# A two-layer gated cross-attention and expert network on one core: who normalises the rows for the second layer's routing

## What is computed

```python
x = x + jnp.tanh(g_xattn[1]) * _L1_xattn_ref(_layernorm(x), ctx_1024, mask, Wq, Wk, Wv, Wo)
x = x + jnp.tanh(g_ffn[1]) * _L1_ffn_ref(_layernorm(x), router_w, w1, w2)

def _layernorm(x, axis=-1, eps=1e-05):
    m = jnp.mean(x, axis=axis, keepdims=True)
    v = jnp.var(x, axis=axis, keepdims=True)
    return (x - m) / jnp.sqrt(v + eps)

# _L1_ffn_ref: 4096 tokens of width 128, 8 experts of width 512, 2 experts a token
logits = xf @ router_w.T
topv, topi = jax.lax.top_k(logits, 2)
topw = softmax(topv)
perm = xf[rev]                       # every token's row twice, sorted by expert
chunks = perm.reshape(e, n * k // e, d)
h = gelu(einsum('ecd,edf->ecf', chunks, w1))
y = einsum('ecf,efd->ecd', h, w2) * sw
out = zeros.at[rev].add(y)
```

## Time and profile before

| what | value |
|---|---|
| median of 3 runs | 753.41 us (750.35 to 755.98) |
| the profiled execution | 759.83 us |
| its span, first to last instruction | 758.3 us |
| busy in the span: TensorE, VectorE, ScalarE, GpSimd | 549.0, 416.8, 231.6, 330.2 us |
| mean granted clock of TensorE | 0.832 of full speed |

### The profile page before, as it was taken

How to read it: one execution, slowest core, us unless ns; L and a number is a source line. 1 busy time by engine, 2 the same in 40 slices (tenths; PEclk the granted TensorE clock), 3 DMA queues, 4 the chain that set the end, 5 groups by cost and what they waited for, 6 DMA issues and landing times.

```text
span 758.3 us, 16967 instructions
## 1 busy us (share of the span) xinstructions
PE 549.0 (72%) x5388; PEld 433.3 (57%) x5389; DVE 416.8 (55%) x1474; ACT 231.6 (31%) x411; POOL 330.2 (44%) x412
## 2 busy tenths in 40 slices
PE   1587957615699999972798887777861388999950
PEld 1356645501289999862354676666650166999950
DVE  4785386997523333314896467878568511222215
ACT  0221001123044444442622454454531021223210
POOL 6212104777535656634500000070747676666650
PEclk9967695865799999996799997786775699999995
DMA  7911000123222222412755164352324113222219
GB/s 199 269 42 32 26 14 30 49 96 99 74 75 82 77 79 74 140 45 68 238 185 175 51 167 109 108 159 51 70 64 129 46 54 103 79 81 77 72 56 311
DMA packets 70254, 74.97 MB, mean 99 GB/s; under 512 B 12216, under 2 KB 58552, under 8 KB 70120
## 3 DMA queue, kind: packets, MB, share of 16 engines
q1 hardware_dynamic: 55240, 49.64, 23.6%
q0 software_dynamic: 9968, 21.88, 9.2%
q10 hardware_dynamic: 4976, 2.53, 1.2%
HBM read 45.62 MB, written 28.29 MB: 97 GB/s over the span
## 4 chain that ended last, share of the span: by engine, by line
PE 51%; DVE 24%; POOL 8%; issue 8%; DMA 6%; ACT 1%; SPq 1%; POOLq 0%; DVEq 0%; ACTq 0%
PE PS L802 47%; POOL xs L543 5%; DVE XN L1406 3%; DVE stats L1385 3%; DMA work<-ys 3%; DVE X L1380 2%; PE PS L983 2%; DVE work L1845 2%; DVE work L1380 1%; POOL work L591 1%; DVE rtmp L1380 1%; DVE mv L1388 1%; DVE nwt L1380 1%; PE PS L1144 1%; POOL work L598 1%
## 5 line engine op out<-in xcount | busy, mean ns | idle before, releaser
L543 POOL DMA_INDIRECT xs<-pack,adr_i x80 | 78.2, 977 | 194.3 <-ACT pack L1219 138.5
L554 POOL DMA_INDIRECT ys<-work x136 | 132.6, 975 | 33.2 <-issue 33.2
L802 PE MATMUL PS<-w,work 128*128 x1088 | 137.4, 281 | 6.5 <-issue 6.4
L802 PEld LDWEIGHTS PS<-w,work 128*128 128x128 f32 x1088 | 129.4, 195 | 11.5 <-issue 10.2
L802 PE MATMUL PS<-work,w1h 128*128 128x256 f16 (+1 forms) x576 | 97.8, 271 | 3.4 <-issue 2.0
L802 PE MATMUL PS<-work 97*64 97x256 f16 (+5 forms) x608 | 75.7, 317 | 13.8 <-DVE work L1512 7.5
L1380 DVE TENSOR_TENSOR work<-PS,work 128x128 f32<-128x128 f32 (+3 forms) x82 | 32.0, 392 | 94.9 <-PE PS L802 50.6
L802 PE MATMUL PS<-work,w1l 128*128 128x256 f16 (+1 forms) x288 | 78.1, 272 | 0.0
L1277 ACT ACTIVATE work<-PS,b 128x256 f32<-128x256 f32 x128 | 50.3, 475 | 77.0 <-PE PS L802 77.0
L802 PEld LDWEIGHTS PS<-work 97*64 97x64 f16 (+2 forms) x608 | 57.7, 165 | 24.7 <-DVE work L1512 10.8
L802 PE MATMUL PS<-ones 128*128 128x512 f16 x195 | 50.7, 418 | 25.7 <-DVE rows_i L1642 12.4
(11 more groups left out here) (288 smaller groups left out, 858.8 us busy)
## 6 DMA issues: line engine op xcount, KB each, us to landing
work<-ys SPq DMA_DIRECT2D x12, 512.0 KB, 6.0
work<-xs SPq DMA_DIRECT2D x32, 130.0 KB
work<-xs SPq DMA_DIRECT2D x60, 65.0 KB
k_parts<-work SPq DMA_DIRECT2D x24, 128.0 KB, 2.1
w<-k_parts SPq DMA_DIRECT2D x8, 384.0 KB
work<-k_parts SPq DMA_DIRECT2D x32, 96.0 KB
work<-q_parts SPq DMA_DIRECT2D x8, 384.0 KB
work<-q_parts SPq DMA_DIRECT2D x32, 96.0 KB
```

What stands on the lines that cost most here:

```text
L543: g.indirect_dma_start(xs[l], bass.IndirectOffsetOnAxis(adr_i[:, k, T:T + 1], 0), pack_of(l, c)[:, s, k, :].bitcast(U32), None)\
L554: g.indirect_dma_start(ys[l], bass.IndirectOffsetOnAxis(xin[:, q, u, :].bitcast(U32)[:, D:D + 1], 0), yrow[:, q, u, :], None).then_inc(ff[ ...
L802: return t.matmul(o, lhsT, rhs, start=start, stop=stop, skip_group_check=True)
```

## The change

The rows of the second layer are no longer normalised by VectorE. GpSimd writes them for the first three groups (chunks 0 to 5) with the same two-step operation on X, mean and 1/std; each group stands in its queue ahead of the scatters of the group's first chunk. ScalarE writes them for the last two groups (chunks 6 and 7) with one activation a tile, x * (1/std) + shift, right before it copies the upper half. For that VectorE computes a shift, -mean/std, after each group's 1/std, and raises a new semaphore `scaled` with it. The first layer keeps its rows on VectorE, and the table of steps stays as it was.

```diff
+        shift_ = sb("shift_", [P, CT_TILES * 2])
...
+        scaled = sem("scaled")
...
+            def rows_normed(p):
+                t = group(1, p)
+                pool.wait_ge(scaled, p + 1)
+                if p >= 2:
+                    pool.wait_ge(pack_lo, NC + t.stop // CT_TILES - 4)
+                for s, T in enumerate(range(t.start, t.stop)):
+                    ins = g.tensor_scalar(XN[:, slots(1, t.start // CT_TILES).start + s, :], X[:, T, 0:D],
+                                          mv[:, T, 0:1], rstd[:, T:T + 1], ALU.subtract, ALU.mult)
+                    if s % CT_TILES == CT_TILES - 1:
+                        ins.then_inc(rt[1]["xn"], 1)
+
             for c in range(NC):
+                if c % 2 == 0 and c < NC - 2:
+                    rows_normed(c // 2)
                 if c < NC // 2:
                     for s in range(CT_TILES):
                         scatter(1, c, (s,))
...
                 for c in route_at("high", g):
+                    if c >= NC - 2:
+                        act.wait_ge(scaled, group_of(1, c) + 1)
+                        act.wait_ge(pack_lo, NC + c - 3)
+                        for s in range(CT_TILES):
+                            T = c * CT_TILES + s
+                            ins = a.activation(XN[:, slots(1, c).start + s, :], X[:, T, 0:D], ACT.Identity,
+                                               bias=shift_[:, s:s + 1], scale=rstd[:, T:T + 1])
+                        ins.then_inc(rt[1]["xn"], 1)
                     route_high(1, c)
...
             def route_rows_normed(l, p):
                 t = group(l, p)
-                if l == 1 and p >= 2:
-                    dve.wait_ge(pack_hi, NC + t.stop // CT_TILES - 4)
                 norm_rows(t, slots(l, t.start // CT_TILES).start, rt[l]["xn"])
...
                 for k in route_at("norm", g):
                     dve.wait_ge(x3_done, group(1, k).stop)
-                    norm_scale(group(1, k))
+                    t = group(1, k)
+                    norm_scale(t)
+                    v_.scalar_tensor_tensor(out=shift_[:, 0:width(t)], in0=mv[:, t, 0], scalar=-1.0, in1=rstd[:, t],
+                                            op0=ALU.mult, op1=ALU.mult).then_inc(scaled, 1)
                     route_lg(1, k)
                 for k in route_at("choose", g):
                     route_choose(1, k)
-                for k in route_at("normed", g):
-                    route_rows_normed(1, k)
```

## The result

The changed kernel took 759.5 us (median of 20 runs, 751.9 to 764.3) where the kernel before took 755.44 (20 runs, 750.35 to 760.13): ratio 1.0058, 95% interval 1.0035 to 1.0082. That is slower by 0.6%, inside the 1% that I called no change; the forecast was +2.0 us, and this comparison gives some +4. The profiled execution took 762.85 us with a span of 761.3 (before 759.83 and 758.3). Two later comparisons of the same kernel gave less; all runs together are at the end of the experiments.

What follows compares the result with a forecast made beforehand. From 561.27 us on, the end was taken to hang on when VectorE and ScalarE have chunk 4 packed. Shift +0.3, port +1.7 and the rest 0 gave +2.0 us on 753.41: 755.4 us, range 750.0 to 760.5.

Steps and rivals of the forecast that it cites:

- Rows removed from VectorE: Taking 32 tiles' normalisations off VectorE gains 0 us, since VectorE then waits for TensorE or GpSimd asks for the table later.
- Shift: One added VectorE instruction a group, before the logits, passed on for three groups at 0.1 us each: +0.3 us.
- GpSimd's normalisation: Each of 24 normalisations of 128 x 128 on GpSimd takes 0.3 us, bounds 0.2 and 1.27; they cost 0 themselves.
- The port: GpSimd's normalisations stretch VectorE's two-input instructions: 1.2 us in group 1's choice, 0.5 in group 0; +1.7 us, bounds 0 and 5.
- The rival that had GpSimd slow and VectorE held up: Each normalisation takes about 1.27 us and delays VectorE some 6 us in groups 0 and 1: 766 us; chance 0.1.
- Group 2 on time: GpSimd's group 2 rows are done at 554.3, some 3 us before ScalarE asks: 0 us.
- late rows: Above 0.7 us per normalisation, group 2 reaches ScalarE late and chunk 4 moves 1 to 2 us: 757 to 758; chance 0.05.
- ScalarE's eight activations: ScalarE's activations for the last two groups take 0.3 us each, 1.2 us for four, and cost 0.
- the idle time 2 us longer: Sign in the changed profile: VectorE idles 2 us longer ahead of each rank result.
- the scatters without a gap from chunk 4 on: Sign in the changed profile: GpSimd's scatters from chunk 4 on follow each other without idle time.
- a chunk 4 some 2 us later: Sign in the changed profile: GpSimd's scatters from chunk 4 on start about 2 us later.
- the change moves nothing: Rival: VectorE takes its turns with GpSimd without loss, leaving only the shift's 0.3 us: 753.7 us; chance 0.25.

Runs made afterwards that it cites:

- e9: The changed kernel measured a third time, with no further edit: 757.07 us (12 runs), ratio 0.9997 to the kernel before.
- e6: Changed kernel with four GpSimd two-input additions of 128 x 512 ahead of group 1's normalisations: 762.6 us (4 runs), ratio 1.0113 to the kernel before.
- e8: Changed kernel with GpSimd's batch for group 2 moved ahead of chunk 3's last four scatters: 760.59 us (12 runs), ratio 1.0051 to the kernel before.
- e1 to e4: Changed kernel again, GpSimd's part alone, ScalarE's part alone, changed kernel with group 2 back on VectorE: ratios 0.9990, 1.0026, 1.0007, 1.0009 to the kernel before.
- e5: Changed kernel with every GpSimd normalisation done twice, first into unread scratch: 760.62 us (6 runs), ratio 1.0100 to the kernel before.

## Why the prediction was right

The total was right, and its largest term was wrong. The measured 759.5 us lies 1.0 us inside the upper bound of 760.5, and 2.0 us of it are the kernel before's own: its median is 755.44 over 20 runs for the 753.41 of the three that I had.

- **Rows removed from VectorE: 0.** Right. The time came back as waits for TensorE in all three large groups (2.61 us to 4.57 in group 1), and the earlier table (597.86 for 599.23) was complete 6.5 us before GpSimd asked for it. In group 0 I had read 1.64 us of cover; with the 0.97 at 481.01 it was 2.61, so that the 0.5 us that I left open there had no ground.
- **Shift: +0.3.** Its size was right: 0.17 us long, the next instruction after 0.09 us (469.63 to 469.72). 0.3 us is below what any comparison here can tell.
- **GpSimd's normalisation: 0.3 us each.** This step failed; it is 0.80. I took the value nearest to the copy. The truth lies between the copy and the sum, inside the bounds of 0.2 and 1.27. A quarter of the sum's elements takes 0.63 of the sum's time, so dividing by elements was the mistake.
- **The port: +1.7.** This step failed. In the choice of group 1, where I had 1.2 us, it is 0 to 0.25 us, and in group 0, where I had 0.5, up to 0.4 (e9). The changed kernel's first profile has none in group 1. The two stretched rows that I had the earlier trace rows were both beside sums with two tensor inputs, and I carried them over to an instruction with one tensor and two scalars per row. e6 shows the difference inside one trace. The rival that had GpSimd slow and VectorE held up needed the port as well and was wrong with it: had the port acted for the whole of each instruction, 0.80 us each would have been near the 0.85 at which it decided the sign.
- **Group 2 on time: 0.** The slack was mis-sized, the price was not. I wrote that it holds up to 0.7 us for one instruction. At 0.80 the rows are late in four of six profiles, ScalarE waiting 0.80 to 1.67 us for them (0.8 us in the mean of the six). The rival "late rows" said so, and said that chunk 4 moves by 1 to 2 us. That part is not seen: the distance from group 2's choice to chunk 4 stays where the versions without these waits have it. (1 to 2 us on top of my 755.4 are 756.4 to 757.4, where the rival has 757 to 758.)
- **ScalarE's eight activations: 0.** Their price was 0.41 us each for 0.3, inside the bounds, and it cost nothing that can be seen (1.0007).

Of the signs that I named, the idle time 2 us longer, the scatters without a gap from chunk 4 on and the early table came. Normalisations of 0.3 us, a choice stretched by 1.2 us and a chunk 4 some 2 us later did not come; it started 0.36 us earlier in the two profiles.

What the rows show of a cost is the shift's 0.3 us and an instruction held up now and then, together 0.3 to some 1.0 us. The runs give +1.8 with an error of 0.7, or +1.1 with an error of 0.6 (above). That the forecast of +2.0 is near them is luck: 1.7 us for the port stood in for the at most 0.7 us that the held-up instructions cost and for a rest that is open, if there is one. My rival "the change moves nothing", at +0.3, does as well by the runs and better by the rows. Open is whether the rest is the clock. In the comparison where the changed kernel was slowest its mean clock was 0.8337, and e8 had 0.8276. But within the 35 runs of before beside e1 to e4 a clock lower by 0.01 goes with 5 us more as well, in one unchanged program. Whether a low clock makes the time long or comes with what does, and whether the place of GpSimd's work moves it, no run here tells apart.

The Trainium skill's page "SBUF — State Buffer", section "Who interferes with whom", lets a GpSimd instruction that reads SBUF shut out VectorE's two-input instructions. By that rule the additions of e6 agree, at 1.05 to 1.70 us for 0.23. The normalisations, which read SBUF too, do not: beside them all but a few such instructions keep their 0.22 to 0.23 us, and in group 1 the longest takes 0.47, which is less than one normalisation of 0.80. Here the measurement decides.

## What to carry to other kernels

Whether GpSimd's work slows VectorE hangs on the form on both sides. Before fearing it, look for that form in a trace, or put it beside the suspected instructions once: e6 needed five lines and gave the answer in single rows, where a ratio with an interval of 0.4% could not. Work moved to an idle engine can be late by where it stands in that engine's queue: e8 took the waits away at the same length. But a wait is not yet a price; follow it to the instruction on which the end hangs, as the distance to chunk 4 does here. And take no difference of 3 us between two profiles as the change's before the unchanged kernel was profiled twice.

## What was not expected of the hardware

- GpSimd's normalisation of 128 x 128 with two scalars per row took 0.80 us in every batch (0.78 at its steadiest, in e5), a sum of four times the elements 1.27 to 1.33 us.
- The form of GpSimd's instruction made the difference for VectorE's 128 x 64 instructions with two inputs: 1.05 to 1.70 us beside sums of two tensors of 128 x 512, 0.21 to 0.23 and at times up to 0.47 beside normalisations of 128 x 128.
- The stretch from the first gather to the end differed by microseconds in one program: 153.7 and 155.2 us in the kernel before, 152.6, 156.4 and 156.8 in the changed one. The gathers were issued at the same pace; the last one of the rows between experts was followed by its store after 2.5 to 2.9 us or after 3.5 to 4.5.
